# A transformer block in split fp32: the experts' gate and up weights stand in TensorE and 512 tokens move, where 128 tokens stood and 352 weight columns moved

## The chip, the cores and the metric

The kernel runs on one core of a Trainium2 chip. The metric is the device time of one execution in microseconds; less is better. The numbers below come from three timed executions of the kernel before and from one profiled execution with its trace.

## The reference, cut to what matters

Four sequences of 1024 tokens with 256 features go through an attention layer (16 heads) and then a feed-forward layer of 8 groups of 8 experts. The change lies in the second:

```python
scores = softmax(x @ gate_w.T)                    # 64 experts per token; top 8 kept in w_e
flat = w_e[:, inv_map]                            # 8 groups x 8
scalar = flat.sum(-1)                             # the mass of a group, per token
soft = softmax(where(flat == 0, -1e9, flat))
xg = x[:, None, :] + einsum('ngi,ghi->ngh', soft, mask_up_w)
g = einsum('ngh,gih->ngi', xg, gate_proj_w)       # 8 groups, 176 inner features each
u = einsum('ngh,gih->ngi', xg, up_proj_w)
a = silu(g) * u
d = einsum('ngi,ghi->ngh', a, down_proj_w)
y = einsum('ng,ngh->nh', scalar, d)               # x + y is the result
```

`x` here is the normalized output of the attention layer. Multiplying the mass into `a` before the down projection gives the same sum over groups.

## The kernel before, in words

Products are taken in fp32r. For precision each operand is split into a high and a low part, and a product is three matmuls: high by high, high by low, low by high (`wth`/`wtl` are the parts of the gate and up weights, `dh`/`dl` of the down weights, `aTh`/`aTl` of the activations; the parts of the normalized tokens lie in the buffers `qh` and `ql`, the soft weights turned in `xq`). All matmuls but transposes are recorded under one line, L46, so that they are told apart by their tiles.

The program is three blocks of engine queues: `attention_prepare`, `attention` (32 head pairs, each a body with an order written out by hand, and a last body LAST that also starts the router of the first tokens) and `ffn`, the experts. Each engine runs its own queue in program order, and semaphores join them.

The experts stage goes over 32 tiles of 128 tokens (`TILES`). Per tile:

- `gate_up(i, g)`, once per group g: six matmuls in which 128 tokens stand and the 352 columns of gate and up weights of the group move, into one PSUM bank (five banks `GB` in turn). `soft(i, q)`, twice per tile, adds the mask product for four groups, in four matmuls of 32 rows each.
- ScalarE takes silu of the gate half into `sg` (`silus`), VectorE multiplies it with the up half and the token's mass, which is one number per partition, into `act_sb` (`gates`, L1819).
- `act_sb` has tokens on partitions; the down projection needs features there. So TensorE turns it in 11 transposes of 128x128 (`transposes`, L1685), ScalarE copies the result as the high part (`high`, L1769), VectorE subtracts for the low part (`low`, L1826), and `down` runs 33 matmuls of 256 columns, whose sum VectorE adds to the tokens (`add_up`, L1834).

The router works on halves of a sequence (`HT` = 4 tiles, 512 tokens; 8 halves). Its steps 0 to 6 on TensorE, 0 to 6 on ScalarE and 0 to 7 on VectorE (`router_tensor`, `router_scalar`, `router_vector`) are laid among the tiles of the half before by the tables `PE_AT`, `ACT_AT` and `DVE_AT`. Step 3 of TensorE turns the selected weights that VectorE's steps 4 and 5 find (top 8 by MAX8, MATCH_REPLACE8); GpSimd normalizes tokens (`router_norm`). The mask products of groups 4 to 7 (`mask_products`) are made once, in tile 0.

SyncE's queue issues all DMAs: loads of tokens (`load`), stores of results (`store`), weights.

## Time and profile before

| | us |
|---|---|
| three timed executions | 1659.49, 1661.84, 1663.2 (median 1661.84) |
| the profiled execution, its own time | 1660.86 |
| its span, first to last instruction | 1658.8 |
| TensorE busy in the span | 1565.8 |
| VectorE, ScalarE, GpSimd busy | 1181.2, 814.4, 806.3 |
| first matmul of the experts stage | at 1160.87 |

A span is counted from the first to the last instruction on the engines; the execution's own time is 2.06 us more. Busy times of TensorE count each matmul from its start until its result is written, and these overlap, so the distance between two starts is what a matmul costs in a row of them, not its duration.

### The profile page before, as it was taken

The numbers are of one execution on the slowest core, as the hardware profiler recorded it, in microseconds if no ns is written. First come the engines' busy times: TensorE is split into PE (matmuls) and PEld (weight loads), VectorE is DVE, ScalarE is ACT, GpSimd is POOL, SyncE is SP. The second block draws the span as 40 slices with busy tenths as digits, with TensorE's granted clock in tenths as the row PEclk, the third lists the DMA queues.
The fourth block names the chain that finished last, engine by engine and source line by source line (L and its number), as shares of the span: only waits on it lengthen the run. The fifth ranks groups of instructions, "written<-read, shape, count | busy, mean of one in ns | idle before, by whom it ended". The sixth has DMA issues, their size and how long they took to land. (4 is left out here: it accounts for less than half of the span.)

```text
span 1658.8 us, 69237 instructions
## 1 busy us (share of the span) xinstructions
PE 1565.8 (94%) x30224; PEld 1343.1 (81%) x30224; DVE 1181.2 (71%) x2780; ACT 814.4 (49%) x1902; POOL 806.3 (49%) x673
## 2 busy tenths in 40 slices
PE   5689999999999999999999999997999999999998
PEld 4568878877778777877877878875899999999998
DVE  6778878887788778878877888886645446445443
ACT  6555555555556555555555555543433333333332
POOL 4376767676667666676767676762010010011000
PEclk9889999999999999999999999998999999999999
DMA  9523221112231112222112311112100000000000
GB/s 299 130 71 79 55 54 45 52 41 73 72 77 53 48 51 77 64 64 73 55 45 63 93 42 42 45 39 77 59 27 1 26 27 1 26 27 1 13 14 13
DMA packets 83981, 91.87 MB, mean 55 GB/s; under 512 B 33696, under 2 KB 58272, under 8 KB 83680
## 3 DMA queue, kind: packets, MB, share of 16 engines
q1 hardware_dynamic: 83680, 87.44, 18.5%
q8 instruction: 240, 3.93, 1.0%
q14 instruction: 61, 0.50, 0.1%
HBM read 55.67 MB, written 14.94 MB: 43 GB/s over the span
## 5 line engine op out<-in xcount | busy, mean ns | idle before, releaser
L1395 ACT ACTIVATE probs<-aps,nmax 128x896 f32<-128x896 f32 (+7 forms) x512 | 378.1, 740 | 410.3 <-DVE nmax L1443 398.4
L1443 DVE CUSTOM_DVE_ANT_0 aps<-aps,mask_row 128x896 f32<-128x896 f32 (+7 forms) x512 | 380.7, 759 | 122.9 <-PE aps L46 119.4
L46 PE MATMUL aps<-kTh,qh 128*128 128x512 f32 (+3 forms) x768 | 291.2, 379 | 13.7 <-DVE ql L1131 7.2
L1122 POOL TENSOR_TENSOR rot<-rot,sinT 64x512 f32<-64x512 f32 x126 | 160.4, 1273 | 292.7 <-DMA rot<-rot 292.7
L46 PE MATMUL aps<-pT_second,vrep 32*64 32x128 f32 (+1 forms) x15616 | 263.5, 260 | 26.2 <-issue 23.3
L46 PEld LDWEIGHTS aps<-pT_second,vrep 32*64 32x64 f32 x15616 | 224.8, 131 | 66.1 <-issue 53.7
L1453 DVE STREAM_TRANSPOSE pT_second<-probs 128x896 f32<-128x896 f32 (+3 forms) x256 | 264.0, 1032 | 4.7 <-ACT probs L1395 4.5
L46 PE MATMUL aps<-kTl,qh 128*128 128x512 f32 (+3 forms) x768 | 259.2, 345 | 1.6 <-issue 1.6
L46 PE MATMUL aps<-kTh,ql 128*128 128x512 f32 (+3 forms) x768 | 223.2, 345 | 0.0
L46 PEld LDWEIGHTS aps<-kTh,qh 128*128 128x128 f32 x768 | 145.5, 189 | 75.0 <-issue 38.9
L1826 DVE TENSOR_TENSOR aTl<-fps,aTh 128x512 fp32r<-128x512 f32 (+1 forms) x96 | 61.9, 646 | 167.3 <-ACT aTh L1769 167.3
L46 PE MATMUL fps<-wth,qh 128*128 128x352 f32 x512 | 176.1, 344 | 3.7 <-PEq L848 3.7
L1769 ACT CAST aTh<-fps 128x512 fp32r<-128x512 f32 (+1 forms) x96 | 52.8, 551 | 235.7 <-PE fps L1685 235.6
L1453 DVE STREAM_TRANSPOSE pT_first<-probs 128x256 f32<-128x256 f32 (+3 forms) x256 | 124.1, 495 | 59.1 <-ACT probs L1395 58.9
L46 PE MATMUL fps<-wtl,qh 128*128 128x352 f32 x512 | 166.1, 324 | 0.0
L46 PE MATMUL fps<-wth,ql 128*128 128x352 f32 x512 | 165.8, 324 | 0.0
L831 POOL TENSOR_SCALAR f_vareps<-f_aggr 128x4 f32<-128x4 f32 x8 | 1.9, 233 | 336.1 <-DVE f_aggr L759 336.1
L1125 POOL TENSOR_TENSOR rot<-rot 64x512 f32<-64x512 f32 x126 | 160.4, 1273 | 9.9
L1131 POOL TENSOR_TENSOR ql<-rot,qh 128x512 fp32r<-128x512 f32 x126 | 159.7, 1285 | 7.4 <-ACT qh L1384 7.4
L1123 POOL TENSOR_TENSOR rot<-rot,cosT 64x512 f32<-64x512 f32 x126 | 161.3, 1280 | 0.0
L46 PEld LDWEIGHTS aps<-kTl,qh 128*128 128x128 f32 x768 | 146.6, 191 | 12.4 <-issue 0.2
L46 PEld LDWEIGHTS aps<-kTh,ql 128*128 128x128 f32 x768 | 137.2, 191 | 8.9
(195 smaller groups left out, 3032.9 us busy)
## 6 DMA issues: line engine op xcount, KB each, us to landing
rot<-rot SPq DMA_DIRECT2D x256, 64.0 KB, 2.5
linv_b<-inverses_scratch SPq DMA_DIRECT2D x128, 128.0 KB
wqs<-wq_scratch SPq DMA_DIRECT2D x30, 256.0 KB, 3.6
raw_numbers<-in_x SPq DMA_DIRECT2D x8, 512.0 KB, 6.4
vrep<-values_scratch SPq DMA_DIRECT2D x16, 256.0 KB, 4.6
inverses_scratch<-linv_t SPq DMA_DIRECT2D x256, 1.0 KB
acc<-in_x SPq DMA_DIRECT2D x16, 256.0 KB, 3.2
x_scratch<-acc SPq DMA_DIRECT2D x16, 256.0 KB, 3.1
```

The source lines that it names most:

```text
L46: return nc.tensor.matmul(out, lhsT, rhs, start=start, stop=stop, skip_group_check=True)
L831: pool.tensor_scalar(t.vareps[:], t.aggr[:, :, 1], EPS, None, ALU.add).then_inc(t.ve, 1)
L1122: eng.tensor_tensor(rot2[:, k, :], rot2[:, k, :], t.sinT[:, cols], ALU.mult).then_inc(q_turned, 1)
L1123: eng.tensor_tensor(rot1[0:64, k, :], rot1[0:64, k, :], t.cosT[0:64, cols], ALU.mult).then_inc(q_turned, 1)
L1125: eng.tensor_tensor(rot1[0:64, k, :], rot1[0:64, k, :], rot2[:, k, :], ALU.add).then_inc(q_add, 1)
L1131: eng.tensor_tensor(ql[:, a, cols], rot1[:, rot_slot(x, r), :], qh[:, a, cols].bitcast(F32), ALU.subtract).then_inc(q_split, 1)
L1395: nc.scalar.activation(probs[:, SLOT[x, r], 0:w], sps[:, at:at + w], ACT.Exp, bias=nmax[:, c, a, j:j + 1], scale=-1.0, accum_out=lsum[:, c ...
L1443: nc.vector.tensor_tensor_reduce(out=s, in0=s, in1=mask[:, N - PW[c][j]:N], scale=-1.0, scalar=3.0e38, op0=ALU.add, op1=ALU.min, accum_out ...
L1453: nc.vector.transpose(pT[c][:, a, 0:w // S32, j * S32:(j + 1) * S32], probs[:, SLOT[EXP(c, a, j), r], 0:w].rearrange("p (b k) -> p b k", k ...
L1769: nc.scalar.copy(aTh[:, i % 2, m.start:m.stop, :].rearrange("p m n -> p (m n)"), turned_in(i, q)[:, 0:len(m) * P]).then_inc(aT_h, 1)
L1826: nc.vector.tensor_tensor(aTl[:, i % 2, m.start:m.stop, :].rearrange("p m n -> p (m n)"), turned_in(i, q)[:, 0:len(m) * P], aTh[:, i % 2, ...
```

## The change

Gate and up weights now stand, 128 features at a time, and the 512 tokens of a half move. The inner features of the 8 groups (8 x 176 = 1408) are taken as 11 blocks of 128 (`MC`); eight blocks lie in one group, and blocks 4, 5 and 10 mix three or four (`MIXED`). A work item n is block m of half H (n = 11 H + m, 88 in all). Its products come out with features on partitions, so the transposes are gone; per item there are 12 products of 512 columns, 2 mask matmuls of 512 columns and full height (4 in block 5), and 12 down matmuls of 256 columns for item n-2 (`LAG`).

With features on partitions the mass of a token is no longer one number per partition. VectorE turns it (32x32 blocks), SyncE stores it to DRAM and loads it back as rows repeated over partitions (`mass_b`, 18 DMAs per half), and GpSimd multiplies it into `sg` (`weigh`), between silu and `gate`. The mask weights are taken in column ranges (256, and 96 for mixed blocks), and GpSimd copies them into zeroed 128-row entries (`mask_clear`, `mask_spread`) that overlie the keys' buffers `kTh`, `kTl`. Down weights are loaded in the last attention body instead of after it. Router steps are laid over the eleven blocks by new tables; in the first half (H = 0) places below 8 are two later and the others one later. VectorE adds the four tiles of a half after all its blocks.

```diff
-PIECES = [(0, 1024), (1024, 2048), (2048, 2560), (2560, KC * 4 * GU)]
-FIRST_QUAD, SECOND_QUAD = (0, 2, 1, 3), (1, 0, 2, 3)
+WORDS = [5 * KC * GB, 6 * KC * GB]
+PIECES = [[(a, min(a + (1024 if a < 2048 else 512), w)) for a in (0, 1024, 2048, 2560) if a < w] for w in WORDS]
+FIRST_QUAD, SECOND_QUAD = (0, 2, 1), (1, 0, 2, 3)
+MIXED = {4: [(0, slice(0, 48), P), (1, slice(48, 96), P), (2, slice(96, P), P)],
+         5: [(2, slice(0, 16), 160), (3, slice(16, 64), P), (4, slice(64, 112), P), (5, slice(112, P), P)],
+         10: [(5, slice(0, 32), 144), (6, slice(32, 80), P), (7, slice(80, P), P)]}
+MEMBERS = [MIXED.get(m, [(m if m < 4 else m - 2, slice(0, P), 0)]) for m in range(MC)]
+SOFT = [[(0, m)] for m in range(5)] + [[(0, 5), (1, 5)]] + [[(1, m)] for m in range(5)]
+DIMS = [g * I + first + r for members in MEMBERS for g, rows, first in members for r in range(rows.stop - rows.start)]
...
+def columns(w, m, k, u):
+    first = ((m % 5 if m < 10 else 5) * KC + k) * GB + u * P
+    return w[m // 5 if m < 10 else 1][:, first:first + P]
...
+def mask_clear(nc, t, q):
+    nc.gpsimd.memset(t.kTh[:, q, :].bitcast(F32), 0.0).then_inc(t.mw_zero, 1)
+    nc.gpsimd.memset(t.kTl[:, q, 0:2 * GB].bitcast(F32), 0.0).then_inc(t.mw_zero, 1)
+def mask_spread(nc, t, q):
+    nc.gpsimd.wait_ge(t.mw_l, q + 1)
+    nc.gpsimd.wait_ge(t.mw_zero, 2 * q + 2)
+    copied = MASK_DONE[4] if q else 0
+    for m in (5, 6, 7, 8, 9, 10) if q else range(5):
...
+            nc.gpsimd.tensor_copy(to, src).then_inc(t.mw_rdy, 1)
+            copied += 1
+            nc.gpsimd.wait_ge(t.mw_rdy, copied)
+MASK_DONE = [sum(len(MEMBERS[k]) for k in range(m + 1)) for m in range(MC)]
+def keep_mass(nc, t, H):
+    nc.sync.wait_ge(t.mass_turned, H + 1)
+    to = t.mass_dram[H % 2].rearrange("g (t a i) -> a (g t) i", a=4, i=32)
+    for a in range(4):
+        nc.sync.dma_start(to[a], t.massT[32 * a:32 * a + 32, :]).then_inc(t.mass_kept, 16)
...
-        dve.tensor_reduce(out=t.mass[:, H % 2].rearrange("p t g -> p (t g)"), in_=fl, axis=AX.X, op=ALU.add)
+        step(dve.tensor_reduce(out=t.mass[:, H % 2].rearrange("p (g t) -> p t g", t=HT),
+                               in_=fl.rearrange("p (t g) s -> p t g s", g=G), axis=AX.X, op=ALU.add))
+        if H > 0:
+            dve.wait_ge(t.mass_kept, 64 * H)
+        dve.transpose(t.massT[:], t.mass[:, H % 2]).then_inc(t.mass_turned, 1)
...
+            sp.wait_ge(t.first_low, len(PIECES[0]))
+            sp.dma_start(t.raw_d, ins["down"].rearrange("(m p) d -> p m d", p=P)).then_inc(t.down_loaded, 16)
+            keep_mass(nc, t, 0)
...
-        DVE_AT = {0: (-5, "after sum"), 1: (-4, "after sum"), 2: (-4, "after sum"), 3: (-3, "before gates"),
-                  4: (-3, "after sum"), 5: (-2, "first"), 6: (-2, "after sum"), 7: (-1, "after sum")}
+        def tok(H):
+            return slice(H % 2 * HN, (H % 2 + 1) * HN)
+        PE_AT = {0: 0, 1: 1, 2: 2, 3: 4, 4: 5, 5: 8, 6: 9}
+        ACT_AT = {0: 0, 1: 1, 2: 3, 3: 4, 4: 6, 5: 8, 6: 9}
+        DVE_AT = {1: 0, 2: 1, 3: 2, 4: 3, 5: 3, 6: 5, 7: 6}
+        def router_parts(at, n):
+            H, m = divmod(n, MC)
+            def place_of(place):
+                if H > 0:
+                    return place
+                return place + 1 if place >= 8 else place + 2
+            return [(H + 1, part) for part, place in at.items() if place_of(place) == m and H + 1 < HALVES]
...
+            def spread_mass(H, m):
+                if H > 0:
+                    sp.wait_ge(weighted, (H - 1) * MC + m + 1)
+                for g, rows, _ in MEMBERS[m]:
+                    row = t.mass_dram[H % 2, g]
+                    sp.dma_start(mass_b[rows, m, :], row.partition_broadcast(rows.stop - rows.start))\
+                        .then_inc(mass_loaded[m], 16)
+            sp.wait_ge(t.mass_kept, 64)
+            for m in range(4):
+                spread_mass(0, m)
             load(2)
             sp.wait_ge(t.x2_stored, 64 * B)
-            sp.dma_start(raw_d[:], ins["down"].rearrange("(m p) d -> p m d", p=P)).then_inc(down_loaded, 16)
+            for m in range(4, MC):
+                spread_mass(0, m)
             for H in range(HALVES - 1):
-                store(H)
-                if H + 3 < HALVES:
-                    sp.wait_ge(x_stored[H % 3], 16 * (H // 3 + 1))
-                    load(H + 3)
+                if H > 0:
+                    store(H - 1)
+                    if H + 2 < HALVES:
+                        sp.wait_ge(x_stored[(H - 1) % 3], 16 * ((H - 1) // 3 + 1))
+                        load(H + 2)
+                keep_mass(nc, t, H + 1)
+                sp.wait_ge(t.mass_kept, 64 * (H + 2))
+                for m in range(MC):
+                    spread_mass(H + 1, m)
...
+            def products(n, u):
+                H, m = divmod(n, MC)
+                if m == 0:
+                    pe.wait_ge(t.xT_l, 2 * H + 2)
+                if n >= 2:
+                    pe.wait_ge((silu_done, act_done)[u], n - 1)
                 for k in range(KC):
+                    for j, (x, w) in enumerate(((t.xTh, t.wth), (t.xTh, t.wtl), (t.xTl, t.wth))):
+                        mm(nc, banks[:, 2 * (n % 2) + u, :], columns(w, m, k, u), x[:, k, tok(H)], k == 0 and j == 0, False)
+            def soft(n, u):
+                H, m = divmod(n, MC)
+                entries = SOFT[m]
+                if u == 0 and m in (0, 5):
+                    pe.wait_ge(t.sT_rdy, 2 * H + (1 if m == 0 else 2))
+                if u == 0 and H == 0:
+                    pe.wait_ge(t.mw_rdy, MASK_DONE[m])
+                for q, e in entries:
+                    last = mm(nc, banks[:, 2 * (n % 2) + u, :], t.mwz[q][e][:, u * P:(u + 1) * P], t.sT[:, q, tok(H)],
+                              False, (q, e) == entries[-1])
+                last.then_inc((gate_ps, up_ps)[u], 1)
+            def down(n):
+                H, m = divmod(n, MC)
+                if H == 0 and m % 4 == 0:
+                    pe.wait_ge(d_l, m // 4 + 1)
+                if m == 0 and H > 0:
+                    pe.wait_ge(o_ready, HT * H)
+                pe.wait_ge(aT_l, n + 1)
+                for i in range(HT):
                     for j, (a, w) in enumerate(((aTh, dh), (aTh, dl), (aTl, dh))):
+                        last = mm(nc, y_of(i), a[:, n % SLOTS, i * P:(i + 1) * P], w[:, m, :], m == 0 and j == 0 and i % 2 == 0,
+                                  m == MC - 1 and j == 2)
+                last.then_inc(d_done, 1)
+            def parts(n):
+                for H, part in router_parts(PE_AT, n):
+                    router_tensor(nc, t, H, part, r_bank)
+            for n in range(TOTAL + LAG):
+                if n == 1:
+                    continue
+                if n == 0:
+                    for k in (0, 1):
+                        products(0, k)
+                    products(1, 0)
+                    router_tensor(nc, t, 0, 5, r_bank)
+                    products(1, 1)
+                    for k in (0, 1):
+                        for u in range(2):
+                            soft(k, u)
+                        if k == 0:
+                            router_tensor(nc, t, 0, 6, r_bank)
+                elif n < TOTAL:
+                    for u in range(2):
+                        products(n, u)
+                        soft(n, u)
+                    parts(n)
+                    if n == 2:
+                        pe.wait_ge(gu_lv, 2)
+                        pe.wait_ge(gu_lp, 2)
+                        mask_products(nc, t, 1, banks[:, 6, :])
+                if n >= LAG:
+                    down(n - LAG)
...
+            def silu(n):
+                act.wait_ge(gate_ps, n + 1)
+                if n >= SLOTS:
+                    act.wait_ge(act_done, n - SLOTS + 1)
+                nc.scalar.activation(sg[:, n % SLOTS, :], banks[:, 2 * (n % 2), :], ACT.Silu).then_inc(silu_done, 1)
+            def high(n):
+                act.wait_ge(act_done, n + 1)
+                if n >= SLOTS:
+                    act.wait_ge(d_done, n - SLOTS + 1)
+                nc.scalar.copy(aTh[:, n % SLOTS, :], act_sb[:, n % SLOTS, :]).then_inc(aT_h, 1)
...
+            def gate(n):
+                dve.wait_ge(up_ps, n + 1)
+                dve.wait_ge(weighted, n + 1)
+                nc.vector.tensor_tensor(act_sb[:, n % SLOTS, :], banks[:, 2 * (n % 2) + 1, :], sg[:, n % SLOTS, :],
+                                        ALU.mult).then_inc(act_done, 1)
+            def low(n):
+                dve.wait_ge(aT_h, n + 1)
+                if n >= SLOTS:
+                    dve.wait_ge(d_done, n - SLOTS + 1)
+                nc.vector.tensor_tensor(aTl[:, n % SLOTS, :], act_sb[:, n % SLOTS, :],
+                                        aTh[:, n % SLOTS, :].bitcast(F32), ALU.subtract).then_inc(aT_l, 1)
+            def add_up(H):
+                dve.wait_ge(d_done, (H + 1) * MC)
+                for i in range(HT):
+                    tile = x2[H % 3][:, i, :]
+                    nc.vector.tensor_tensor(tile, y_of(i), tile, ALU.add).then_inc(o_ready, 1)
...
+            for n in range(TOTAL):
+                gate(n)
+                if n > 0:
+                    low(n - 1)
...
+                parts(n)
+                if n % MC == LAG - 1 and n > MC:
+                    add_up(n // MC - 1)
+            low(TOTAL - 1)
+            add_up(HALVES - 1)
...
+            def weigh(n):
+                H, m = divmod(n, MC)
+                pool.wait_ge(silu_done, n + 1)
+                pool.wait_ge(mass_loaded[m], 16 * len(MEMBERS[m]) * (H + 1))
+                nc.gpsimd.tensor_tensor(sg[:, n % SLOTS, :], sg[:, n % SLOTS, :], mass_b[:, m, :], ALU.mult)\
+                    .then_inc(weighted, 1)
+            mask_spread(nc, t, 0)
             pool.wait_ge(t.soft_rdy, 2)
             second_quad_low()
...
+            pool.wait_ge(gu_lv, 2)
+            pool.wait_ge(gu_lp, 2)
+            mask_clear(nc, t, 1)
+            for n in range(TOTAL):
+                H, m = divmod(n, MC)
+                weigh(n)
+                if n == 3:
+                    pool.wait_ge(weighted, 4)
+                    mask_spread(nc, t, 1)
+                if m in (9, 10) and H + 2 < HALVES:
+                    if m == 9:
+                        router_root(nc, t, H + 2)
+                        pool.wait_ge(t.xT_ps, 2 * H + 4)
+                    for i in range(2 * (m - 9), 2 * (m - 9) + 2):
+                        router_norm(nc, t, H + 2, i)
```

What TensorE's queue holds near the end of a tile before, around the last transposes (`act_sb` turned by `ident` into a PSUM bank, then the down matmuls):

```order
L46 MATMUL fps<-wth,qh 128x352
L46 MATMUL fps<-wtl,qh 128x352
L46 MATMUL fps<-wth,ql 128x352
L1685 MATMUL fps<-ident,act_sb 128x128 x3
L46 MATMUL fps<-dh,aTh 128x256
L46 MATMUL fps<-dl,aTh 128x256
L46 MATMUL fps<-dh,aTl 128x256
```

And now, at the end of block 4 of a half (the standing operand is named last; `kTl` holds a mask entry, `mask_row` the selected weights of the router):

```order
L47 MATMUL fps<-qh,wtl 128x512
L47 MATMUL fps<-ql,wth 128x512
L47 MATMUL fps<-xq,kTl 128x512
L767 MATMUL fps<-ident,mask_row 128x128 x2
L47 MATMUL fps<-dh,aTh 128x256
L47 MATMUL fps<-dl,aTh 128x256
L47 MATMUL fps<-dh,aTl 128x256
```

The transposes of activations are gone from between products and down matmuls, the products are 512 wide, and router step 3 stands directly behind block 4's last mask matmul.

VectorE's queue around the router steps 4 and 5 before: step 4 (L774 to L778) in one tile, step 5 (L782, L785) at the head of the next, with a low part and four gates between:

```order
L1819 SCALAR_TENSOR_TENSOR act_sb<-fps,mass,sg 128x176 x4
L1834 TENSOR_TENSOR x_0<-fps,x_0 128x256
L774 TENSOR_REDUCE r<-mask_row 128x4
L775 RECIPROCAL r<-r 128x4
L776 TENSOR_TENSOR mask_row<-mask_row,r 128x256
L63 MEMSET f_spot_v 1x1
L778 MAX top<-mask_row 128x8 x4
L63 MEMSET f_spot_v 1x1
L1826 TENSOR_TENSOR aTl<-fps,aTh 128x512
L1819 SCALAR_TENSOR_TENSOR act_sb<-fps,mass,sg 128x176 x4
L782 MATCH_REPLACE mask_row<-top,mask_row 128x64 x4
L785 TENSOR_TENSOR mask_row<-mask_row 128x256
```

And now, in block 3 of a half: the gate of item n, the low part of item n-1, then both router steps, then the next gate:

```order
L1885 TENSOR_TENSOR act_sb<-fps,sg 128x512
L1892 TENSOR_TENSOR aTl<-act_sb,aTh 128x512
L842 TENSOR_REDUCE r<-mask_row 128x4
L843 RECIPROCAL r<-r 128x4
L844 TENSOR_TENSOR mask_row<-mask_row,r 128x256
L64 MEMSET f_spot_v 1x1
L846 MAX top<-mask_row 128x8 x4
L64 MEMSET f_spot_v 1x1
L850 MATCH_REPLACE mask_row<-top,mask_row 128x64 x4
L853 TENSOR_TENSOR mask_row<-mask_row 128x256
L1885 TENSOR_TENSOR act_sb<-fps,sg 128x512
```

Steps 4 and 5 now stand together in one block, and TensorE's step 3, which needs the result of the second, stands at the end of the block after.

## Rows read from the trace of the kernel before

**Rows 1.** The page, part 1: busy time of each engine, share of the span, instructions

```profile
PE 1565.8 (94%) x30224; PEld 1343.1 (81%) x30224; DVE 1181.2 (71%) x2780; ACT 814.4 (49%) x1902; POOL 806.3 (49%) x673
```

**Rows 2.** The chain that ended last, in order of time: start, us, what

```profile
1238.55 5.74 PE fps L46 x43
...
1300.09 5.74 PE fps L46 x43
...
1627.08 6.90 PE fps L46 x49
...
1641.16 6.90 PE fps L46 x49
```

**Rows 3.** Windows: stretch, its us, busy us of each engine, granted clock, DMA

```profile
1238.55:1300.09 61.54, 60.93 (x447) 57.30 (x446) 31.51 (x93) 22.38 (x55) 6.81 (x6) 1.00 0.06 18
...
1160.00:1180.00 20.00, 18.16 (x127) 15.25 (x128) 15.27 (x25) 10.53 (x21) 3.38 (x2) 0.91 0.46 141
```

**Rows 4.** Timeline, TensorE, experts stage, tiles 30 and 31: start, us, engine, line

```profile
1629.85 0.28 PE L46 MATMUL fps<-dh,aTh 128*128 128x256 f32 x1
...
1630.91 0.32 PE L46 MATMUL fps<-wth,qh 128*128 128x352 f32 x1
...
1633.82 0.60 PE L1685 MATMUL fps<-ident,act_sb 128*128 128x128 f32 x4
...
1634.35 0.44 PE L46 MATMUL fps<-mw,xq 32*128 32x352 f32 x4
...
1634.71 0.43 PE L46 MATMUL fps<-wth,qh 128*128 128x352 f32 x1
...
1634.98 0.32 PE L46 MATMUL fps<-wtl,qh 128*128 128x352 f32 x1
```

**Rows 5.** Timeline, TensorE, attention: first and last of four 512-column products

```profile
622.89 0.39 PE L46 MATMUL aps<-kTl,qh 128*128 128x512 f32 x1
...
623.59 0.62 PE L46 MATMUL aps<-kTh,ql 128*128 128x512 f32 x2
```

**Rows 6.** Groups with shapes kept apart, 1180 to 1658 us: busy, mean ns, idle before

```profile
L735 ACT CAST xq<-fps 128x512 fp32r<-128x512 f32 x14 | 8.2, 589 | 15.8 <-PE fps L715 15.8
L763 DVE TENSOR_TENSOR ql<-fps,qh 128x512 fp32r<-128x512 f32 x12 | 8.2, 685 | 11.7 <-ACT qh L723 11.7
```

**Rows 7.** Groups with shapes kept apart, GpSimd, whole run

```profile
L1131 POOL TENSOR_TENSOR ql<-rot,qh 128x512 fp32r<-128x512 f32 x126 | 159.7, 1285 | 7.4 <-ACT qh L1384 7.4
```

**Rows 8.** Timeline, router steps of one half, ScalarE and VectorE

```profile
1249.80 1.28 ACT L726 ACT_TABLE_LOAD   x1
...
1251.54 0.42 DVE L774 TENSOR_REDUCE r<-mask_row 128x4 f32<-128x256 f32 x1
...
1253.34 0.06 DVE L63 MEMSET f_spot_v<- 1x1 f32 x1
...
1257.86 0.08 DVE L782 MATCH_VALUE_LOAD mask_row<-top,mask_row 128x8 f32 x1
...
1258.76 0.42 DVE L785 TENSOR_TENSOR mask_row<-mask_row 128x256 f32<-128x256 f32 x1
```

**Rows 9.** Timeline, start of the experts stage

```profile
1160.87 0.40 PE L46 MATMUL fps<-wth,qh 128*128 128x352 f32 x1 [3.68 <-PEq L848]
...
1162.84 2.94 DVE L807 TENSOR_TENSOR rot<-mask_row,soft_h 128x256 f32<-128x256 f32 x2
...
1163.00 2.50 POOL L1874 TENSOR_TENSOR wtl<-raw_numbers,wth 128x1024 fp32r<-128x1024 f32 x1 [11.53 <-DVE rot L804]
...
1168.58 0.80 PE L46 MATMUL fps<-wth,mu 128*32 128x352 f32 x8
...
1171.09 0.43 PE L46 MATMUL fps<-wth,qh 128*128 128x352 f32 x1
```

**Rows 10.** Timeline, the last instruction of VectorE

```profile
1656.16 0.42 DVE L1834 TENSOR_TENSOR x<-fps,x 128x256 f32<-128x256 f32 x1 [2.37 <-PE fps L46]
```

**Rows 11.** DMA issues: transfer, queue, count, KB each, us from issue to landing

```profile
vrep<-values_scratch SPq DMA_DIRECT2D x16, 256.0 KB, 4.6
```

More of the change, by code:

```diff
@@ L29 @@
 GU = 2 * I
+GB = 2 * P
 QC = 512
@@ L616, in mask_products @@
     for n, (k, part) in enumerate([(k, part) for k in range(KC) for part in (t.wth, t.wtl)]):
[L617 to L620 removed]
+        for g, m, first, width, at in mask_windows(q):
+            to = bank[32 * (g % 4):32 * (g % 4) + 32, at:at + 2 * width].rearrange("p (u c) -> p u c", u=2)
+            last = mm(nc, to, t.mu4[:, k, g, :], both_columns(part, m, k, slice(first, first + width)).bitcast(F32),
+                      n == 0 and at == 0, n == 3)
     last.then_inc(t.mw_ps, 1)
@@ L1800, in _ @@
+            high(TOTAL - 1)
         @block.vector
```

354 lines of the change are left out of this document (117 added, 237 removed).

## Prediction

> **What bounds the kernel now.** I read the page first. TensorE is busy in 94% of the span, VectorE in 71%, the other two in 49% [rows 1]. Then the chain that ended last, in order of time: in the experts stage it is TensorE pieces and little else, and they repeat, 61.54 us from 1238.55 to 1300.09 and 14.08 us from 1627.08 to 1641.16 [rows 2]. The first distance is a half (four tiles) with router steps, the second one tile without. The window over the first half has the granted clock at 1.00, TensorE busy 60.93 of 61.54 us, VectorE 31.51, ScalarE 22.38, GpSimd 6.81 [rows 3]. So the stage is paid in TensorE's slots, and the other engines have half their time or more free. What a slot costs is the distance between starts. Four tiles are 56.32 us, so the router of a half costs 61.54 - 56.32 = 5.22 us.
>
> Slots in the experts stage [rows 4]: nine down matmuls of 256 columns from 1629.85 to 1630.91, 0.118 each; eighteen products of 352 columns from 1630.91 to 1633.82, 0.162 each. Both are 0.46 ns per column. Four transposes and the switch to the next kind take 1633.82 to 1634.35, 0.53; four 32-row mask matmuls 0.36; the first product behind them 0.27 instead of 0.16. At 512 columns the stage has no row. By its rate of 0.46 ns a column it would be 0.235; three spacings in attention give 0.70/3 = 0.233 [rows 5]. I take 0.235.
>
> **What the change does to TensorE.** Products per half: before 4 tiles x 48 x 0.162 = 31.0; after 11 x 12 = 132 x 0.235 = 31.0. The columns are the same number, so turning the experts gives nothing there. Down matmuls, 132 x 0.118 = 15.6, are the same too. Mask matmuls: before 8 groups of four x 0.36 = 2.9; after 24 x 0.235 = 5.6, so a loss of 2.7. Transposes: before 4 x (two sets of four at 0.53, one of three at about 0.44) = 6.0, after nothing. The remaining switches (0.11 behind each mask group, 0.1 ahead of it) are about 0.8 per half, also gone. By the whole period, which catches what such a list misses: before 56.32, after 31.02 + 5.64 + 15.58 = 52.24. The gain is 4.08 per half, 32.6 for eight halves. The router's own matmuls are unchanged, 5.22 per half.
>
> **The waits that come in.** Call U the moment when the slot of an item's last mask matmul ends; items are 3.29 (products and mask) + 1.41 (down) = 4.71 apart. ScalarE's silu of 512 columns is taken as the 512-column copy, 0.59, VectorE's gate as L763, 0.69 [rows 6], GpSimd's weigh as 128x512 with two inputs, 1.29 [rows 7]. The gate half is complete 1.65 before U and is seen 0.2 later, silu ends at U - 0.8, weigh at U + 0.55, gate at U + 1.3, the low part of the item before at U + 2.0. That low part is needed by the down matmuls at the next U, 4.7 later: a slack of 2.7. Products wait for the gate of two items back, which has more than 6 us. So the plain loop has no stall, and weigh, though new, lies beside TensorE.
>
> Router steps are the narrow place. In block 3 the Exp waits behind silu and the high part and needs a table load of 1.28 and then some 0.42, as the 256-wide VectorE row: it ends at about U + 1.5, before VectorE is free at U + 2.0. Step 4 took 1251.54 to 1253.40 = 1.86, step 5 1257.86 to 1259.18 = 1.32 [rows 8]. They end at U + 5.2, and TensorE asks for the result at U + 4.7. A wait of 0.5, in seven halves 3.5 us. Behind it on TensorE stand the down matmuls, which then start as much later. The other steps have a block or more between giver and taker. GpSimd in block 9 has weigh, root and two norms, about 5.4 us against 4.7, made good in block 10.
>
> The start: TensorE has been idle 3.68 us [rows 9], and the granted clock of the first 20 us is 0.91 [rows 3], so about 3.6 us at the lower level (1.2 instead of 2.4 GHz); it costs some 1.6 us before and after alike. Before, the rest of the start is the mask products of groups 4 to 7, 1168.58 to 1171.09 = 2.5 [rows 9]; with 448 columns for 352 they are 3.3. New is that the first weigh stands in GpSimd's queue behind seven mask copies, two weight subtractions (2.50 for 1024 columns [rows 9], 1.3 for 512) and two clears. I put it at 1172 to 1173, which holds the products of item 2 for about 1; silu of item 0, behind a router copy, holds them for another 1. In all the start's overhead over a steady run: before 4.7, after 8.2 (1.6 + 3.3 + 0.9 for router steps 5 and 6 + 2.4 of waits). The end: tile 31 began at 1634.71 and had 14.08 us, so 1648.79; its down matmuls need 3.9, and the last sum starts at 1656.16 [rows 4, 10]. So 3.3 us of waits there, which go, since two items lie between product and down. But VectorE now adds four tiles at the end instead of one, 1.1 more. Mass DMAs: 18 per half, of up to 256 KB; a load of that size from scratch landed in 4.6 [rows 11]. In the first half, the tightest, the mass is stored around block 7 and needed four blocks (19 us) later; store and load are some 10. They queue on SyncE behind the store of the half before last, which is on time. The earlier load of the down weights takes a DMA out of the start, where nobody waited for it: nothing.
>
> **The sum.** -32.6 (body) + 3.5 (router) + 3.5 (start) - 3.3 + 1.1 (end) = -27.8. The profiled execution itself took 1660.86, so 1633.1; the median of the timed ones is 1.0 above it. I forecast **1634 us**.
>
> A rule that speaks on the 512-column slot. The Trainium skill, TensorE: Matmul & The Clock Gate, section Back-to-back issue gap, gives the gap of a warm matmul as columns/2.4 plus 2.5 ns: 216 ns at 512, but also 149 at 352 and 109 at 256. The trace does not agree at 352 and 256 (162 and 118). By that rule the 1248 matmuls of 512 columns would be 1248 x 0.019 = 24 us cheaper, and the time 1610; that is the far end of rival C.
>
> **Rivals.**
> - *A, the forecast:* the body gains 4.08 a half, the router waits 0.5. Own range 1628 to 1641. Chance 0.50.
> - *B, the elementwise chain is later than the sum of its rows.* At the start a two-input VectorE instruction (L807, 0.42 each by its kind) was stretched so that two took 2.94, ending just behind GpSimd's 2.50 us subtraction [rows 9]. Weigh is such a GpSimd instruction, once per item, and the low part and the router's differences are such VectorE instructions. If each half loses 1.29 in block 3 and as much once more, and the start 2, it is 7 x 1.9 to 2.6 + 2: 1648 or so, still faster. Against: in the plain block weigh ends before gate starts. Chance 0.22. The Trainium skill, GPSIMD Engine Reference, section 1. Specifications, says the same of the two engines: they share SBUF interfaces, with contention for VectorE instructions with two SBUF inputs; this row agrees.
> - *C, wide matmuls cost less per column* than the stage's 0.46 ns, with the long stream of tokens: at 0.22 a slot it is -19, 1615. The attention rows (0.233) are against it; nothing in the stage shows it. Chance 0.14.
> - *D, slower: weigh is on the path.* Every product waits for the gate of two items back and every down for the low part. If silu, weigh, gate, high and low outgrow the slack of 2.7, the excess is paid 88 times. It decides from 27.8/88 = 0.32 beyond the slack, a chain longer by 3.1: weigh at 4.3 instead of 1.29, or the mass not there. At 1 us of excess it is about 1722. The weigh row is a firm one of 126. Chance 0.07.
> - *E, B and D in part cancel the gain:* no change, 1661. Chance 0.03. What is left, 0.04, goes to a body that gains more through fewer switches, near 1626.
>
> **Numbers.** What a measurement of this kernel can tell from none is about 0.2% (3.3 us). A, B, C and the rest are faster by more: 0.90; same 0.03; slower 0.07. Bounds: the 512-column slot between 0.225 and 0.238 is -12 to +4 us; the router's waits between 0 and 2.6 a half -4 to +15. The range that leaves out D, E and the ends of B and C is 1617 to 1650.
>
> **What would show it.** In the changed profile: 512-column products 0.235 apart; a period of 57.5 to 58 us per half with router steps and 52.2 in the last, without; VectorE's result of step 5 ending about 0.5 behind block 4's last mask matmul, and TensorE idle there by that much in each half; weigh near 1.29, ended before the gate starts; the first weigh near 1172; no idle time of TensorE ahead of the last down matmuls. The forecast is wrong if the slot differs from 0.235 by 0.01 (12 us), if TensorE waits in blocks without router steps (rival D), or if the lost time of block 3 is over 1 us.

## The result and the profile after

| | before | after |
|---|---|---|
| timed executions, median (lowest to highest) | 1660.66 us (1659.18 to 1663.2), 4 | 1635.55 us (1629.72 to 1637.05), 4 |
| ratio, with 95% interval | | 0.9841 [0.9813, 0.9868] |
| profiled execution, own time / span | 1660.86 / 1658.8 | 1635.59 / 1633.5 |
| first matmul of the experts stage | 1160.87 | 1163.76 |
| experts stage, from there to the end of the span | 497.9 | 469.7 |

The forecast was 1634 us, with a range of 1617 to 1650. The kernel is 1.6% faster. A second set of four executions of the same kernel, measured later, gave 1631.19 us and a ratio of 0.9848 [0.9827, 0.9869].

The page of the changed kernel: busy time of each engine, the chain's shares of the span, and the group of the new weigh product. The line after them is the chain of the kernel before.

```profile
PE 1533.4 (94%) x29424; PEld 1279.1 (78%) x29424; DVE 1160.9 (71%) x2609; ACT 801.9 (49%) x1725; POOL 928.2 (57%) x783
...
PE 13%; issue 8%; POOL 6%; DVE 2%; ACT 0%; POOLq 0%; DVEq 0%
...
L1939 POOL TENSOR_TENSOR sg<-sg,mass_b 128x512 f32<-128x512 f32 x88 | 114.8, 1304 | 291.1 <-ACT sg L1837 290.8
```

```profile
PE 27%; DVE 2%; ACT 0%; issue 0%
```

Beside [rows 1], TensorE has 32.4 us less and GpSimd 121.9 more, 114.8 of it weigh. The chain now names GpSimd, where before it was TensorE nearly alone. It is easy to read too much into this: the chain goes back through whatever released an engine last, and TensorE is idle hardly anywhere in the stage. The period says what the stage costs. Three rows of the chain in time order, at the same place of three halves in a row, and the window over one half:

```profile
1253.10 20.14 PE fps L47 x114
...
1310.82 20.14 PE fps L47 x114
...
1368.55 20.15 PE fps L47 x114
```

```profile
1253.10:1310.82 57.72, 57.02 (x332) 49.38 (x332) 29.05 (x73) 20.85 (x33) 20.47 (x17) 1.00 0.22 69
```

A half takes 57.73 us instead of 61.54 [rows 2]; TensorE is busy 57.02 of it, at a granted clock of 1.00 as before [rows 3]. GpSimd went from 6.81 to 20.47 and is still free two thirds of the time.

TensorE waits once in such a half, in front of router step 3. TensorE's timeline there (start, duration, line, tiles), then VectorE's and GpSimd's:

```profile
1251.33 0.40 PE L47 MATMUL fps<-ql,wth 128*128 128x512 f32 x1
1251.56 0.40 PE L47 MATMUL fps<-xq,kTl 128*128 128x512 f32 x1
1252.66 0.44 PE L767 MATMUL fps<-ident,mask_row 128*128 128x128 f32 x2 [0.70 <-DVE mask_row L853]
```

```profile
1251.36 0.21 DVE L850 MATCH_REPLACE8 mask_row<-top,mask_row 128x64 f32<-128x64 f32 x1
1251.60 1.00 DVE L853 TENSOR_TENSOR mask_row<-mask_row 128x256 f32<-128x256 f32 x1
```

```profile
1251.03 1.29 POOL L1939 TENSOR_TENSOR sg<-sg,mass_b 128x512 f32<-128x512 f32 x1 [3.40 <-ACT sg L1837]
```

The products are 0.23 apart. The 0.70 of idle is counted from the modelled end of the matmul before; counted in slots, the transpose would have started at 1251.79 and started at 1252.66, 0.87 late. The last VectorE step in front of it, L853, takes 1.00 while GpSimd's weigh runs beside it until 1252.32. By kind, over the plain part of the stage:

```profile
L879 DVE TENSOR_TENSOR rot<-mask_row,soft_h 128x256 f32<-128x256 f32 x14 | 13.0, 969 | 0.0
...
L853 DVE TENSOR_TENSOR mask_row<-mask_row 128x256 f32<-128x256 f32 x7 | 7.2, 1030 | 0.2
...
L767 PE MATMUL fps<-ident,mask_row 128*128 128x128 f32 x14 | 3.1, 300 | 4.9 <-DVE mask_row L853 4.9
...
L844 DVE TENSOR_TENSOR mask_row<-mask_row,r 128x256 f32<-128x256 f32 x7 | 3.0, 425 | 0.2
```

L844 is the same kind of instruction with no weigh beside it: 425 ns against 1030 and 969. (Both kinds have two inputs in SBUF.)

The attention part did not stay as it was. From the 27.8 us forecast for the whole, the stage alone gave 28.2 and the profiled execution as a whole 25.3. TensorE's timeline in the last body of attention, in router step 4, and the first product of the experts stage:

```profile
1150.55 1.33 PE L47 MATMUL aps<-onehot,wselT 128*128 128x64 f32 x5 [0.46 <-ACT wselT L797]
1154.14 0.69 PE L47 MATMUL aps<-onehot,wselT 128*128 128x64 f32 x3 [2.26 <-issue]
...
1163.76 0.47 PE L47 MATMUL fps<-qh,wth 128*128 128x512 f32 x1 [3.33 <-PEq L920]
```

Eight equal matmuls with all their operands there are parted by 2.26 us in which the trace shows nothing that TensorE waited for. The moved load of the down weights, 1.4 MB, was issued at 1145.95, and its traffic ended at about 1152.

### The profile page after: what moved, and what is told of

The parts are those of the page before. It is cut to its first block and busy times, and to the rows that moved or that the text cites. A ratio compares the mean times of both kernels' runs of the same rounds, so it can differ in the third digit from the quotient of the medians.

```text
span 1633.5 us, 68004 instructions
## 1 busy us (share of the span) xinstructions
PE 1533.4 (94%) x29424; PEld 1279.1 (78%) x29424; DVE 1160.9 (71%) x2609; ACT 801.9 (49%) x1725; POOL 928.2 (57%) x783
## 3 DMA queue, kind: packets, MB, share of 16 engines
q1 hardware_dynamic: 98640, 110.65, 23.5%
## 5 line engine op out<-in xcount | busy, mean ns | idle before, releaser
L1939 POOL TENSOR_TENSOR sg<-sg,mass_b 128x512 f32<-128x512 f32 x88 | 114.8, 1304 | 291.1 <-ACT sg L1837 290.8
L1885 DVE TENSOR_TENSOR act_sb<-fps,sg 128x512 f32<-128x512 f32 x88 | 60.6, 689 | 230.3 <-PE fps L47 179.6
L1837 ACT ACTIVATE sg<-fps 128x512 f32<-128x512 f32 x88 | 52.5, 597 | 247.7 <-PE fps L47 247.7
L47 PE MATMUL fps<-qh,wth 128*128 128x512 f32 x352 | 140.4, 399 | 4.3 <-PEq L920 3.3
L47 PE MATMUL fps<-qh,wtl 128*128 128x512 f32 x352 | 140.2, 398 | 0.0
L47 PE MATMUL fps<-ql,wth 128*128 128x512 f32 x352 | 139.3, 396 | 0.0
```

The source lines that it names most:

```text
L47: return nc.tensor.matmul(out, lhsT, rhs, start=start, stop=stop, skip_group_check=True)
L1837: nc.scalar.activation(sg[:, n % SLOTS, :], banks[:, 2 * (n % 2), :], ACT.Silu).then_inc(silu_done, 1)
L1885: nc.vector.tensor_tensor(act_sb[:, n % SLOTS, :], banks[:, 2 * (n % 2) + 1, :], sg[:, n % SLOTS, :], ALU.mult).then_inc(act_done, 1)
L1939: nc.gpsimd.tensor_tensor(sg[:, n % SLOTS, :], sg[:, n % SLOTS, :], mass_b[:, m, :], ALU.mult)\
```

## The experiments

Lengths are taken inside one profile (the stage, or a stretch between two named instructions), since the place at which the stage starts moves between executions: it lies between 1159.5 and 1167.4 in the eight profiles whose programs are equal until there.

### The load back at its old place

```diff
-            sp.wait_ge(t.first_low, len(PIECES[0]))
-            sp.dma_start(t.raw_d, ins["down"].rearrange("(m p) d -> p m d", p=P)).then_inc(t.down_loaded, 16)
```

The second line stands in the experts' SyncE queue again, behind the wait for `x2_stored`.

> The change with one part undone: the down weights are loaded at the start of the experts stage again, after the stores of the last attention body. In the changed kernel the last attention body (from the reciprocal of the last row sums to the first matmul of the experts) took 31.86 us where it had 30.36 before, and TensorE stood 2.26 us in the middle of router step 4 with nothing to wait for that the profile shows, while the DMA engines moved the down weights. Theory 1: that load takes DMA time from what feeds TensorE (its instructions): without it the idle 2.26 is gone, the body takes 29.6 to 30.4 us, the whole is 1.5 to 2.3 us less than the changed kernel, ratio to before about 0.983. Rival: the 1.5 us come from the mask products in narrower pieces and the mass steps (turn, store) ahead of the stage; then the body stays at 31.9 and the time does too. Second rival: the load is now late for the first down matmuls, which would cost 1 us or more at item 2.

Measured 1635.4 us (1629.38 to 1638.78), ratio 0.9866 [0.9845, 0.9888]: as the changed kernel. The parts differ, though. TensorE in the last body, and at the first down products:

```profile
1151.71 1.97 PE L47 MATMUL aps<-onehot,wselT 128*128 128x64 f32 x8 [0.46 <-ACT wselT L797]
```

```profile
1182.98 0.35 PE L47 MATMUL fps<-dh,aTh 128*128 128x256 f32 x1 [3.09 <-DVE aTl L1891]
1183.17 0.28 PE L47 MATMUL fps<-dl,aTh 128*128 128x256 f32 x1
1183.29 0.33 PE L47 MATMUL fps<-dh,aTl 128*128 128x256 f32 x1
1183.43 0.41 PE L47 MATMUL fps<-dh,aTh 128*128 128x256 f32 x1
1183.64 0.42 PE L47 MATMUL fps<-dl,aTh 128*128 128x256 f32 x1
```

The eight one-hot matmuls run in one piece, 10.62 us from the first of them to the stage instead of 13.21; the whole last body, from the reciprocal of the last row sums to the stage, has 30.21 instead of 31.87, as expected. But the down weights come late: 3.09 us of waiting, and matmuls 0.21 apart behind it instead of 0.12. The stage has 474.3 us, 4.6 more. So the second rival holds beside the theory, and the whole gained nothing. The move of the load, priced at nothing, has two effects: it costs 1.7 to 2.6 us in attention, and it saves 4.6 in the stage. The 2 to 3 us between them are less than the two medians can tell apart.

### Step 3 later

```diff
-            def parts(n):
+            def parts(n, late=False):
...
-                    router_tensor(nc, t, H, part, r_bank)
+                    if (part == 3) == late:
+                        router_tensor(nc, t, H, part, r_bank)
...
+                if n < TOTAL:
+                    parts(n, late=True)
```

TensorE's step 3 is taken behind the twelve down matmuls of its block instead of ahead of them.

> The change with TensorE's router step 3 behind the down matmuls of its block instead of ahead of them (1.4 us later), nothing else. In the changed kernel TensorE waited 0.7 us for VectorE's step 5 in each of seven halves, 4.9 us in all. Theory: that wait is the only thing there, so it goes whole: 4 to 5 us less than the changed kernel, the period of a half 57.0 instead of 57.73, ratio to before about 0.981. Rival: the wait moves on (ScalarE's copy of the turned weights and TensorE's step 4 come later and wait in block 5, or the silu queued behind that copy is late): period 57.7, no gain.

Measured 1624.26 us (1622.2 to 1625.58), 0.9801 [0.9779, 0.9823]. The chain, two halves:

```profile
1248.41 18.71 PE fps L47 x102
...
1305.22 18.71 PE fps L47 x102
```

The period is 56.81, 0.92 less, and the wait is gone; the stage is 463.3 us, 6.4 less, which is 7 x 0.92. L853 is still stretched (1044 ns), but no one waits for it. The wait cost what the slots say (0.87), not the 0.70 of the idle column. To settle whether the 11 us between the medians were more than that, both ran again on one chip, with these expectations:

> The changed kernel unchanged, for a comparison on the same chip with the versions of this call: 0.984 of the kernel before, and 6 to 11 us above the version with step 3 late.

> The version with step 3 late once more, on the same chip as the changed kernel: by the profiles 7 halves x 0.92 us = 6.4 us faster than that. A difference near 11 us as in the separate runs would mean that something outside the seven halves also changed.

Measured 1631.19 (1630.01 to 1634.11) and 1625.79 (1623.37 to 1629.03): 5.4 apart, with stages of 469.7 and 463.3. So the step is worth 6.4, and the rest of the 11 was the spread of the attention part between executions.

### Both

The two edits together.

> Both edits of the two runs beside it. If the two are apart, the gains add up: 6 to 7 us less than the changed kernel, ratio to before 0.980. If the load of the down weights cannot be moved back without a wait at the first down matmuls, or the last body keeps its 31.9 us, only the 4 to 5 us of the step remain.

Measured 1627.13 us (1624.91 to 1630.5), 0.9822 [0.9799, 0.9845]; stage 465.2, with 2.4 us of waits for `aTl` and 1.6 for `act_sb`; one-hot matmuls in one piece, 11.76 us to the stage. The gains did not add up to the 6 to 7 us expected: the profile keeps the late step's gain, and the load at its old place is no gain with it either. It costs 1.9 us in the stage here, where it cost 4.6 without the late step; the load landed 9.6 us after its issue in this execution and 12.6 in the other, which is about that difference.

### A small weigh product

```diff
-                nc.gpsimd.tensor_tensor(sg[:, n % SLOTS, :], sg[:, n % SLOTS, :], mass_b[:, m, :], ALU.mult)\
+                nc.gpsimd.tensor_tensor(sg[:, n % SLOTS, 0:64], sg[:, n % SLOTS, 0:64], mass_b[:, m, 0:64], ALU.mult)\
```

It leaves the mass out for 448 of 512 tokens.

> The change with GpSimd's weighing cut to 64 of the 512 tokens of an item (the mass is left out for the other 448, so the result is another): one instruction per item remains, of some 0.3 us instead of 1.30. My forecast: weighing lies beside TensorE, so the plain blocks do not move (12 products, masks and down matmuls in 4.7 us); only where it stretches VectorE (the last difference of step 5, 1.03 us instead of 0.42) the wait for step 5 falls from 0.7 to about 0.1 to 0.3. So 3 to 4 us less than the changed kernel, plus up to 1 us at the start. Rival D of the prediction, weighing on the path: more than 10 us less.

Measured 1625.47 us (1621.38 to 1625.97), 0.9805 [0.9782, 0.9827]; stage 461.3. The groups:

```profile
L1939 POOL TENSOR_TENSOR sg<-sg,mass_b 128x64 f32<-128x64 f32 x85 | 28.0, 329 | 361.0 <-ACT sg L1837 361.0
...
L879 DVE TENSOR_TENSOR rot<-mask_row,soft_h 128x256 f32<-128x256 f32 x14 | 5.3, 417 | 0.0
...
L853 DVE TENSOR_TENSOR mask_row<-mask_row 128x256 f32<-128x256 f32 x7 | 3.1, 438 | 0.2
```

With weigh short, L853 and L879 are back at 438 and 417 ns, the wait for step 5 is gone, and the period is 56.82, the same as with the late step. That is more than the expectation had, which left 0.1 to 0.3 of the wait. So the wait comes from weigh, and in two ways. In the half at 1251, counted from the start of block 4's last mask matmul, step 5 ended at 1.04 in the changed kernel and ends at 0.07 here. Of these 0.97 us, 0.57 are the stretch of L853, and the other 0.4 were there before the router steps began: the gate of block 3, which waits for weigh and stands ahead of them, starts at -4.27 instead of -3.84. The other 2.0 us of this stage lie outside the seven halves, at the start and the end.

### A longer weigh

```diff
+                    nc.gpsimd.tensor_tensor(spare_w[:], sg[:, n % SLOTS, :], mass_b[:, m, :], ALU.mult).then_inc(spare_done, 1)
```

This stands once ahead of each weigh product in the first kernel, and twice in the second; nothing reads `spare_w`.

> The changed kernel with one extra 128x512 multiply of GpSimd (into a spare buffer, nothing reads it) ahead of each weigh product in the experts stage: sg is 1.3 us later, GpSimd has 1.3 more for each of 88 items. My theory (what is left on the path are TensorE's slots, and the weigh product ends 2.7 us before the down products want it): no wait of the gate for TensorE in the plain blocks, period of a half with a router block at most 1 us longer (step 3 and step 5 are a little later), time +0 to +8 us. Rival (the weigh product is on the path of every item): +1.3 x 80 = +104 us.

> As the run before, with two extra multiplies: 2.6 us later, GpSimd busy 3.9 us for each item of about 4.7 us. My theory says that the slack of 2.7 us is just used up: time +5 to +40 us, with waits of TensorE on the activations between down products. The rival gives +208 us.

Measured 1662.97 us (1655.7 to 1668.78), 1.0007 [0.9989, 1.0026], for one extra; 1766.84 us, one execution, for two. One extra costs 30.4 us in the stage, far more than my 0 to 8 and far less than the rival's 104. Two cost 131 us in all, where 5 to 40 were expected and 208 by the rival. TensorE's waits from the start of the stage on (in all, times, longest), and VectorE's stretched groups:

```profile
PE fps L767 <- DVE mask_row L853: 15.5, 7, 2.2
PE fps L751 <- POOL cosT L912: 4.9, 5, 1.0
...
PE fps L783 <- DVE rot L879: 3.1, 1, 3.1
PE fps L47 <- DVE aTl L1894: 1.7, 1, 1.7
PE fps L47 <- DVE act_sb L1887: 1.6, 1, 1.6
```

```profile
L866 DVE TENSOR_TENSOR mask_row<-mask_row,r 128x256 f32<-128x256 f32 x7 | 10.5, 1501 | 0.2
...
L853 DVE TENSOR_TENSOR mask_row<-mask_row 128x256 f32<-128x256 f32 x7 | 8.2, 1175 | 0.2
```

In the 88 items TensorE waited once for `act_sb` and once for `aTl`: a chain longer by 1.3 is within the slack of 2.7 of the plain items, as forecast. What pays are the router's steps, 23.5 us of the 26.8 in these rows, 5.7 of which (4.9 at L767, 0.8 at L783) the changed kernel has too. Most of the rest is the clock. Windows of this kernel (stretch, length, busy times of TensorE, its weight loads, VectorE, ScalarE and GpSimd, granted clock, DMA share, GB/s) around a wait of 2.24 us that ended at 1320.88, and two down matmuls behind it, 0.21 apart, show it:

```profile
1310.00:1320.00 10.00, 8.64 (x46) 7.02 (x44) 6.20 (x25) 5.20 (x7) 4.79 (x4) 1.00 0.16 52
...
1322.00:1330.00 8.00, 8.00 (x45) 7.22 (x44) 0.44 (x2) 1.11 (x2) 2.57 (x2) 0.84 0.01 2
1330.00:1345.00 15.00, 15.00 (x87) 13.00 (x86) 11.04 (x19) 7.00 (x10) 8.18 (x6) 1.00 0.48 142
```

```profile
1322.04 0.41 PE L47 MATMUL fps<-dl,aTh 128*128 128x256 f32 x1
1322.25 0.41 PE L47 MATMUL fps<-dh,aTl 128*128 128x256 f32 x1
```

The lower clock lasts from 1321.13 to 1324.54. It does not follow every such wait: of the six waits of 2.23 to 2.24 us in front of step 3, four have it and two, ended at 1260.4 and 1444.7, do not. The halves tell the price. Of the five in the middle, three take 61.9 to 62.0 us, where the clock fell, and two 60.5, where it did not, so it costs 1.5 us each time.

With two extra, the plain items wait too (12 times for `aTl`, 11.9 us), and router step waits come to 70 us; the mean granted clock of the stage is 0.92.

### Short mask products

```diff
-                for q, e in entries:
-                    last = mm(nc, banks[:, 2 * (n % 2) + u, :], t.mwz[q][e][:, u * P:(u + 1) * P], t.sT[:, q, tok(H)],
-                              False, (q, e) == entries[-1])
+                q, e = entries[-1]
+                last = mm(nc, banks[:, 2 * (n % 2) + u, 0:HN // 4], t.mwz[q][e][:, u * P:(u + 1) * P],
+                          t.sT[:, q, tok(H)][:, 0:HN // 4], False, True)
```

It leaves out three quarters of the mask products, and one of the two entries of block 5.

> The changed kernel with the mask products cut to 128 of their 512 columns and to one entry in the block that has two; it leaves out part of the mask products. The mask product of the changed kernel costs a slot of 0.233 us; 128 columns should cost about 0.06 to 0.07. 8 x 22 slots at 0.165 less, and 16 slots gone at 0.233: about -33 us, if TensorE's slots alone set the stage. If the stage were held by GpSimd or VectorE (rival), less than half of that comes.

Measured 1611.44 us, one execution; stage 444.1, 25.6 less where 33 were expected. A short one and its neighbours:

```profile
1253.13 0.39 PE L47 MATMUL fps<-ql,wth 128*128 128x512 f32 x1
1253.36 0.22 PE L47 MATMUL fps<-xq,kTl 128*128 128x128 f32 x1
1253.41 0.45 PE L47 MATMUL fps<-qh,wth 128*128 128x512 f32 x1
1253.71 0.39 PE L47 MATMUL fps<-qh,wtl 128*128 128x512 f32 x1
```

The short matmul itself takes 0.05, but the product behind it has 0.30 instead of 0.23: together 0.35 instead of 0.47, a saving of 0.12 and not 0.165. 176 x 0.12 + 16 x 0.233 = 25 us. TensorE's slots set the stage; no new wait came, and those that were there grew by 1.9 us in all.

### The kernel before with few transposes

```diff
-                for m in blocks(q):
+                for m in (blocks(q) if i < 2 or i == TILES - 1 else blocks(q)[-1:]):
```

It leaves out all but one transpose of each set in tiles 2 to 30.

> The kernel before with one transpose of a set instead of four or three in tiles 2 to 30 (it leaves out the other transposes, so the rest of a set is stale): 29 x 8 = 232 transposes fewer. My prediction priced what the change saves in transposes at 6.0 us of 7.3 per half. If a transpose costs about 0.09 us on TensorE's path: -21 us. Rival (they lie in gaps that TensorE had anyway): under -5 us.

Measured 1639.45 us, one execution; stage 474.2 instead of 497.9, so 23.7 us for 232 transposes, 0.10 each. The term of 6.0 per half had 0.09 for one more transpose in a set, so its main part is confirmed; what a whole set costs beyond that, the switch behind it, this run does not price. (The 7.3 per half of the expectation stands nowhere in the prediction, whose gains are 6.0 and 0.8.) At 0.10 each the 352 transposes of all tiles are 36 us, an estimate, against which the change pays 8 x 2.7 for wider mask products.

### The load behind the mass

```diff
-            sp.wait_ge(t.first_low, len(PIECES[0]))
-            sp.dma_start(t.raw_d, ins["down"].rearrange("(m p) d -> p m d", p=P)).then_inc(t.down_loaded, 16)
             keep_mass(nc, t, 0)
+            sp.wait_ge(t.first_low, len(PIECES[0]))
+            sp.dma_start(t.raw_d, ins["down"].rearrange("(m p) d -> p m d", p=P)).then_inc(t.down_loaded, 16)
```

On top of the late step 3.

> The version with step 3 late, with the load of the down weights issued behind the four stores of the mass instead of ahead of them, some 12 us later (at about 1158 instead of 1146 on the time base of the changed kernel); it would land at about 1166, and ScalarE's first copy from it comes at 1173. My theory (this load's traffic holds up the fetching of TensorE's instructions in the middle of the last body's router step 4): the eight one-hot products run without the idle 2.0 to 2.3 us between them, last body 30.2 to 30.6 us instead of 31.5, no wait for aTl at the first down products, 1.0 to 1.5 us faster than the version with step 3 late alone. Rival (the gap is TensorE's own and has nothing to do with the load): last body unchanged at 31.5. A second rival: the hold-up only moves, to the start of the experts stage, and the gain there is lost again.

Measured 1623.62 us (1621.63 to 1626.48), 0.9801 [0.9779, 0.9822]; beside it on the same chip the late step alone had 0.9814 [0.9791, 0.9837]. TensorE's timeline, this kernel and then the one with the late step alone:

```profile
1150.63 1.97 PE L47 MATMUL aps<-onehot,wselT 128*128 128x64 f32 x8 [0.46 <-ACT wselT L797]
...
1161.13 0.65 PE L47 MATMUL fps<-qh,wth 128*128 128x512 f32 x1 [3.46 <-PEq L920]
```

```profile
1147.75 1.33 PE L47 MATMUL aps<-onehot,wselT 128*128 128x64 f32 x5 [0.46 <-ACT wselT L797]
1150.79 0.69 PE L47 MATMUL aps<-onehot,wselT 128*128 128x64 f32 x3 [1.71 <-issue]
...
1160.39 0.48 PE L47 MATMUL fps<-qh,wth 128*128 128x512 f32 x1 [3.31 <-PEq L920]
```

The load now goes out at 1155.11. The gap is gone, 10.50 us to the stage instead of 12.64, the stage stays 463.3, and no down product waits for its weights. That keeps both advantages. By the profiles it is 2.1 us from the first one-hot matmul on, and 3.0 for the whole last body; the medians are 2.2 apart, but their intervals overlap, so the profiles alone show it. Its median is the lowest of all versions that leave nothing out.

What stands in the gap, the traces can narrow down, though no experiment was made for it. They have a DMA queue of a kind of its own, "instruction", and its queue 8 moves packets of 16 KiB (16384 bytes each, 233 of them in the changed kernel). The DMA queues in one window, 1146 to 1151.4, of the kernel before and then of the changed one:

```profile
q8 instruction: 1, 0.02, 1.5%
```

```profile
q1 hardware_dynamic: 1282, 1.31, 77.2%
```

Before, a packet came in this window; in the changed kernel the load had the DMA engines to itself until 1151.4. The times of single packets in the traces, beside the stop in front of the sixth one-hot matmul:

| | packet before, start | next packet | sixth one-hot starts | after the packet's end | idle |
|---|---|---|---|---|---|
| changed kernel | 1144.54 | 1151.51 to 1152.59 | 1154.14 | 1.55 | 2.26 |
| one extra weigh | 1147.71 | 1151.24 to 1152.55 | 1154.07 | 1.52 | 0.81 |
| before, few transposes | 1146.15 | 1149.71 to 1150.97 | 1152.32 | 1.35 | 0.3 |
| before | 1144.21 | 1147.69 to 1149.03 | 1150.79 | 1.76 | none |
| load behind the mass | 1144.79 | 1148.24 to 1149.20 | 1151.76 | 2.56 | none |

In the eight profiles with the load ahead of step 4 TensorE stops here, always in front of the same matmul, and goes on 1.28 to 1.55 us after the end of a packet. In seven of them the stop is 1.7 to 2.5 us, and the packet starts 6.2 to 7.0 us after the one before it; in all other profiles that distance is 3.4 to 3.8. The eighth, with one extra weigh, has a packet in time and a stop of 0.81: its load moved only from 1151 on, and its one-hot matmuls ran 0.11 apart instead of 0.21. And the kernel before with few transposes stops for 0.3 at the same place without any load. So a late packet makes the long stop, but a short one can come without the load. In the seven profiles the last body takes 31.5 to 33.4 us, in the six others 28.8 to 30.6.

The rule is wider than this gap. In the 13 profiles TensorE has 253 idle times over 0.6 us that end in "issue", with a packet of queue 8 ahead of them, in the kernel before as well. Each of the 253 ended 1.17 to 1.70 us after the end of such a packet, a band in which only about 11% of all matmuls start. In the kernel before, these idle times come to 24 us of the whole. The Trainium skill, Runtime: NRT & Kernel Launch, section Instruction fetch mechanics, says that a sequencer fetches its instructions through a DMA queue of its own, in blocks of 16 KiB, and that this is mostly hidden. The blocks agree with the packets, and the times agree with TensorE waiting for them; "mostly hidden" fails wherever such an idle time stands. That the load ahead of step 4 brings the long stop is shown by moving it away three times. That the late packet is the link is read from the times alone.

## Why the prediction held, point by point

- **The 512-column slot,** 0.235, was 0.233. The rate per column carried over from 352 and 256 columns to 512, and rival C (0.22) fell. The formula for an isolated matmul on the page TensorE: Matmul & The Clock Gate, section Back-to-back issue gap, in the Trainium skill (216 ns) would have put the kernel at 1610; the trace does not agree.
- **The body,** 56.32 to 52.24. The last half has no router steps. Its gates start 4.70 apart, and 4.92 twice around block 5 (VectorE's timeline below); ten distances from 1577.33 to 1624.78 and one more of 4.70 are 52.15. Right to 0.1, and its two terms hold: a transpose at 0.10 by the run with few of them, and a mask product near a slot by the two distances of 4.92, which are 0.44 above two plain ones for the two more mask products of block 5.

```profile
1596.13 0.69 DVE L1885 TENSOR_TENSOR act_sb<-fps,sg 128x512 f32<-128x512 f32 x1 [3.41 <-PE fps L47]
1601.05 0.69 DVE L1885 TENSOR_TENSOR act_sb<-fps,sg 128x512 f32<-128x512 f32 x1 [3.63 <-PE fps L47]
1605.97 0.69 DVE L1885 TENSOR_TENSOR act_sb<-fps,sg 128x512 f32<-128x512 f32 x1 [3.63 <-PE fps L47]
```

- **The router's matmuls,** said to be unchanged at 5.22 per half. Without the wait a half takes 56.81, so they cost 56.81 - 52.15 = 4.66. The step was mis-sized by 0.56 a half, 3.9 us in seven. The trace of the kernel before shows where it lay: the 5.22 are the difference of two periods and were taken for matmuls, but TensorE waited in that half for `aTl`, 0.61 us, and in five other halves for 0.59 to 0.61. The change took that wait away.

```profile
1285.68 0.39 PE L46 MATMUL fps<-dh,aTh 128*128 128x256 f32 x1 [0.61 <-DVE aTl L1826]
```

- **The wait for step 5,** forecast 0.5 per half, was 0.92. Place and cause were right, the size was not, since step 5 was taken at the 1.32 of [rows 8]. I had seen the stretch at the start of the stage [rows 9] and given it to rival B, instead of asking which VectorE instruction lies beside the weigh of block 4. The error of 2.9 us and the one above nearly cancel: 5.58 per half instead of 5.72.
- **Start and end.** Seven periods and a last half were 7 x 61.54 + 56.32 = 487.1 of 497.9 before, and are 7 x 57.73 + 52.15 = 456.3 of 469.7 after. So start and end together grew from 10.8 to 13.4, by 2.6 where +1.3 was forecast (+3.5 - 3.3 + 1.1). The 3.3 of waits that I took to be there at the end before were only 1.03 and 1.07 in the trace, so 1.2 less could go. The waits at the start that I put at 2.4 show as idles of 0.8, 0.7 and 0.3; the first weigh started 9.9 us into the stage, not 11 to 12. At the end the last down matmuls wait 0.38, and the span ends 4.2 after the last sums start instead of 2.6 [rows 10], so the four sums cost 1.6 and not 1.1.
- **Weigh** takes 1.30 and is off the path of the plain items: +1.3 on it left them without a wait. In block 3 it is on the path, since the gate there waits for it ahead of the router steps. Rival D needed 3.1 more; at +2.6 it has begun.
- **The down load,** priced at nothing "where nobody waited for it". This step was wrong twice, as told above, with +1.7 to +2.6 and -4.6. I had asked only who waits for the load, not what its traffic meets where it goes.
- **Rival B** was half right: its mechanism, in block 3, is what the small weigh product shows. Its price of 1.9 to 2.6 per half was not reached, since only the instructions that overlap a weigh are held.
- **The total** is in part luck. The stage alone gave 28.2 for the 27.8 forecast, with errors inside it that nearly cancel; and the attention part, which the forecast left as it was, took 2.9 us longer in the profiled execution and moves by more than that from one execution to the next.

## What to carry to other kernels

When work goes to GpSimd, list which VectorE instructions with two SBUF inputs will run beside it, and price those at up to their duration plus GpSimd's (an estimate from the rows above), where another engine waits for their result. A step that waits for such a chain is moved behind work that is ready, at no cost: here 6.4 us for four lines. And a big load that "nobody waits for" still has a place: put it where its traffic meets least, and late enough only for its first reader.

## What the runs showed of the hardware

- A VectorE instruction of 128x256 with two SBUF inputs took 425 ns alone, 969 to 1044 ns beside GpSimd's product of 128x512 and up to 1501 where two such products ran in a row, and was back at 417 and 438 ns when that product was cut to 64 columns. The Trainium skill, GPSIMD Engine Reference, section 1. Specifications, names such a contention; these runs agree and add its size.
- An idle of 2.24 us in an otherwise full TensorE can be followed by a granted clock of 0.84 in the next 8 us, with 256-column matmuls 0.21 apart instead of 0.12: the lower of the two levels, 1.2 for 2.4 GHz, for about 3.4 us. That adds 1.5 us to the wait. Two of six such waits were not followed by it, and behind the waits of 0.70 the clock stayed at 1.00.
- A short matmul (128 columns) passes on part of its saving to the one behind it: 0.05 and 0.30, where two long ones have 0.233 each.
- A load of 1.4 MB (350 to 390 GB/s) ahead of a stream of ready matmuls was followed by a stop of 1.7 to 2.5 us in seven of eight profiles. TensorE's idle times over 0.6 us with nothing to wait for ended 1.17 to 1.70 us after a 16 KiB packet of kind "instruction", in 253 of 253 cases.
